# An mLSTM and feed-forward kernel on one core: the gate rows' broadcast in four transfers, and another order of calls on all engines

## What is computed

```python
def block(x, ctx):
    q, k, v = layernorm(x), ctx, ctx                # 4 heads of 128
    ig, log_fg = gates(q, k, v)                     # per row and head
    cums = cumsum(log_fg)
    log_D = cums[s] - cums[t] + ig[t]               # for t <= s
    m = max_t(log_D)
    C = (q @ k.T / sqrt(128)) * exp(log_D - m)
    h = C @ v / (max(|sum_t C|, exp(-m)) + 1e-6)    # per head
    x = x + headnorm(h) * outnorm_weight
    y = layernorm(x)
    g = silu(bitlinear(y, w_gate)) * bitlinear(y, w_up)    # 512 -> 2048
    return x + bitlinear(g, w_down)                 # 2048 -> 512
```

## Time and profile before

| | us |
|---|---|
| median of 3 runs | 712.29 |
| lowest, highest | 709.3, 714.63 |
| profiled execution, own time | 717.73 |
| its span, first to last instruction | 716.0 |
| PE busy (matmuls) | 595.0 (83%) |
| DVE busy | 532.6 (74%) |
| ACT busy | 495.5 (69%) |
| POOL busy | 302.6 (42%) |
| mean granted TensorE clock | 0.95 |

### The profile page before, as it was taken

How to read it: one execution, slowest core, us unless ns; L and a number is a source line. 1 busy time by engine, 2 the same in 40 slices (tenths; PEclk the granted TensorE clock), 3 DMA queues, 4 the chain that set the end, 5 groups by cost and what they waited for, 6 DMA issues and landing times. The chain is left out here.

```text
span 716.0 us, 12756 instructions
## 1 busy us (share of the span) xinstructions
PE 595.0 (83%) x3630; PEld 385.9 (54%) x3630; DVE 532.6 (74%) x1390; ACT 495.5 (69%) x812; POOL 302.6 (42%) x489
## 2 busy tenths in 40 slices
PE   1816548798898889898898889897999989789996
PEld 1806435376456655565456645664656655456442
DVE  3159477767987688857897798869886699689863
ACT  1877864687758766777659776877577775875652
POOL 1126455554444535535435445444444356144200
PEclk9999658899999999989999999999998999999999
DMA  8763414000142111510242123310160031000001
GB/s 337 310 232 127 171 73 164 16 27 20 75 162 75 45 69 38 204 44 0 74 161 73 44 74 100 135 44 7 68 219 30 15 148 44 19 13 15 32 15 45
DMA packets 30752, 63.75 MB, mean 89 GB/s; under 512 B 2304, under 2 KB 18816, under 8 KB 27136
## 3 DMA queue, kind: packets, MB, share of 16 engines
q1 hardware_dynamic: 30144, 62.92, 24.2%
q10 hardware_dynamic: 576, 0.44, 0.3%
HBM read 54.84 MB, written 8.52 MB: 88 GB/s over the span
## 5 line engine op out<-in xcount | busy, mean ns | idle before, releaser
L556 PE MATMUL GU<-WQ,xqT 128*128 128x512 bf16 x1024 | 245.3, 388 | 4.4 <-DVE FF L1153 4.3
L556 PEld LDWEIGHTS GU<-WQ,xqT 128*128 128x128 bf16 x1024 | 99.7, 100 | 109.2 <-issue 12.5
L586 PE MATMUL ACC<-WQ,FF 128*128 128x512 bf16 x512 | 117.4, 383 | 2.2 <-ACT FF L818 2.2
L799 ACT ACTIVATE FF<-GU,cgu 128x512 f32<-128x512 f32 x128 | 86.4, 688 | 25.2 <-PE GU L556 23.2
L1153 DVE TENSOR_TENSOR FF<-FF,GU 128x512 f32<-128x512 f32 x128 | 85.2, 681 | 12.0 <-ACT FF L799 8.7
L807 ACT ACTIVATE FF<-FF,magic,hs 128x1024 f32<-128x1024 f32 x64 | 78.7, 1237 | 15.7 <-DVE hs L1184 15.7
L586 PEld LDWEIGHTS ACC<-WQ,FF 128*128 128x128 bf16 x512 | 50.0, 99 | 59.4 <-ACT FF L818 2.6
L504 PE MATMUL AT<-vext,CT 128*128 128x129 f32 x256 | 56.5, 306 | 6.1 <-ACT gate_parts L697 3.8
L571 PE MATMUL TPB<-ident,FF 128*128 128x128 bf16 x512 | 40.2, 223 | 23.4 <-DVE FF L1195 18.8
L765 ACT ACTIVATE work<-AT,pb 128x128 f32<-128x128 f32 x128 | 47.8, 450 | 13.9 <-POOL pb L1448 13.3
L1455 POOL TENSOR_TENSOR work<-work,norm_bc 128x512 f32<-128x512 f32 x32 | 41.8, 1305 | 35.9 <-ACT work L765 35.9
(11 more groups left out here) (114 smaller groups left out, 1234.1 us busy)
## 6 DMA issues: line engine op xcount, KB each, us to landing
bc<-gate_rows SPq DMA_DIRECT2D x8, 2048.0 KB, 7.5
xin<-in_x SPq DMA_DIRECT2D x32, 256.0 KB, 2.8
kT<-in_ctx_t SPq DMA_DIRECT2D x8, 1024.0 KB, 4.9
vext<-in_ctx SPq DMA_DIRECT2D x32, 256.0 KB, 3.7
out<-FF SPq DMA_DIRECT2D x32, 256.0 KB, 2.3
WQ<-in_w_gate SPq DMA_DIRECT2D x4, 1024.0 KB, 12.6
FF<-in_w_up SPq DMA_DIRECT2D x4, 1024.0 KB, 15.3
FF<-in_w_down SPq DMA_DIRECT2D x4, 1024.0 KB, 4.7
```

The costliest lines, as they stand in the source:

```text
L556: last = nc.tensor.matmul(dst, xqT[:, b, P * k:P * (k + 1)], w[:, k, 512 * j:512 * (j + 1)], start=(k == 0), stop=(k == KC - 1))
L586: last = nc.tensor.matmul(ACC[:, :], hT[:, b % 2, P * k:P * (k + 1)], WD[:, k, :], start=(k == 0), stop=(k == JT - 1))
L799: nc.scalar.activation(sg[:, j % 2, :], GU[:, 2 * (j % 2), :], ACT.Silu, scale=cgu[:, b, 0:1]).then_inc(silu_done, 1)
```

## The change

The broadcast of the gate rows becomes four calls spread_rows(g, b), each with the four rows of a batch (512 KB on the chip), a semaphore of its own and a wait for its own batch's last readers only. Its readers (exp_decay, weigh_q) wait for their batch; exp_rows waits for all four. spread_small is split into keep_floor(g) and keep_decay(g, b). The lists of calls are written in another order on all five engines; the two ring tables are written from another starting point, and their cyclic order is the same. The work and the depth of the pipeline are the same.

```diff
-        bc_in = sem("bc_in")
+        bc_in = [sem(f"bc_in{b}") for b in range(B)]
...
 
-            def spread_rows(g):
...
-                rows_out_at, ct_ready_at = values(sp, (g + 1) * 16, g * 4)
+            def spread_rows(g, b):
+
+                if absent(g):
+                    return
+                n = g * 4 + b
...
-                             rows_dram.rearrange("r n -> (r n)").partition_broadcast(P)).then_inc(bc_in, 16)
+                r = slice(NH * b, NH * (b + 1))
+                sp.dma_start(bc[:, r, :, :].rearrange("p r k t -> p (r k t)"),
+                             rows_dram[r, :].rearrange("r n -> (r n)").partition_broadcast(P)).then_inc(bc_in[b], 16)
 
...
-                if absent(g):
-                    return
-                dve.wait_ge(bc_in, (g + 1) * 16)
-                V.tensor_copy(decay[:, :], bc[:, :, 1, P - 1]).then_inc(dve_seq, 1)
+            def keep_floor(g):
+                if absent(g):
+                    return
+                V.tensor_copy(floor_n[:, :], cols[:, 2, :]).then_inc(dve_seq, 1)
                 count.next()
-                V.tensor_copy(floor_n[:, :], cols[:, 2, :]).then_inc(dve_seq, 1)
+
+            def keep_decay(g, b):
+                if absent(g):
+                    return
+                dve.wait_ge(bc_in[b], (g + 1) * 16)
+                r = slice(NH * b, NH * (b + 1))
+                V.tensor_copy(decay[:, r], bc[:, r, 1, P - 1]).then_inc(dve_seq, 1)
                 count.next()
```

The order on SP (a part), and on POOL:

```diff
+                step = step_of(it)
                 oldest, former, now, coming = it - 2, it - 1, it, it + 1
+                load_x(now, 3)
+                spread_rows(former, 3)
                 load_x(coming, 0)
+                if step == 0:
+                    load_weights(0, w_gate)
+                load_v(former, 3)
+                if step == 0:
+                    load_weights(1, w_up)
                 if step == 1:
                     load_quarter(2, w_down, 0)
                     load_quarter(2, w_down, 1)
                     load_quarter(2, w_down, 2)
                     load_quarter(2, w_down, 3)
+                load_k(coming)
                 load_v(now, 0)
-                if step == 0:
-                    load_weights(1, w_up)
+                spread_rows(now, 0)
+                spread_rows(now, 1)
+                store(oldest, 0)
                 load_x(coming, 1)
-                load_k(coming)
+                load_v(now, 1)
+                store(oldest, 1)
                 load_x(coming, 2)
-                store(oldest, 1)
-                load_v(now, 1)
-                spread_rows(now)
-                load_x(coming, 3)
+                spread_rows(now, 2)
                 store(oldest, 2)
+                store(oldest, 3)
                 load_v(now, 2)
-                if step == -1:
-                    load_weights(0, w_gate)
-                load_v(now, 3)
-                store(oldest, 3)
-                store(former, 0)
 
             for it in range(-1, FULL):
                 iteration(it)
...
+                weigh_keys(former, 2)
+                head_scale(former, 1)
                 x_rstd(coming, 0)
-                head_scale(former, 1)
+                mask_scores(now, 1)
                 residual(former, 1, slot_former)
                 weigh_keys(former, 3)
                 x1_rstd(former, 1)
                 head_scale(former, 2)
+                mask_scores(now, 2)
                 residual(former, 2, slot_former)
-                weigh_keys(now, 0)
                 x1_rstd(former, 2)
                 head_scale(former, 3)
-                x_rstd(coming, 1)
+                weigh_q(now, 0)
                 residual(former, 3, slot_former)
                 x1_rstd(former, 3)
-                weigh_q(now, 0)
                 weigh_q(now, 1)
+                weigh_keys(now, 0)
+                x_rstd(coming, 1)
                 x_rstd(coming, 2)
+                mask_scores(now, 3)
                 x_rstd(coming, 3)
+                weigh_q(now, 2)
+                head_scale(now, 0)
+                weigh_q(now, 3)
+                residual(now, 0, slot_now)
                 mask_scores(coming, 0)
-                weigh_q(now, 2)
+                x1_rstd(now, 0)
                 weigh_keys(now, 1)
-                mask_scores(coming, 1)
-                head_scale(now, 0)
-                weigh_keys(now, 2)
-                weigh_q(now, 3)
-                mask_scores(coming, 2)
-                residual(now, 0, slot_now)
-                x1_rstd(now, 0)
-                mask_scores(coming, 3)
```

More of the change, by code:

```diff
@@ L1274, in iteration @@
+                state_update(former, 2)
+                multiply(former, 0, 2)
+                copy_hT(oldest, 3)
                 if step == 0:
                     weight_round(0, 0)
-                x1_scale(former, 1, slot_former)
-                copy_cols(now)
-                multiply(former, 0, 1)
+                x_norm(coming, 0, slot_coming)
+                if step == 0:
+                    weight_round(0, 1)
+                x1_stats(former, 2, slot_former)
                 if step == 0:
@@ L1291, in iteration @@
                 h_scale(former, 0)
-                x1_scale(former, 2, slot_former)
-                if step == 0:
-                    weight_round(0, 2)
-                multiply(former, 1, 0)
                 multiply(former, 1, 1)
                 x1_stats(former, 3, slot_former)
+                x1_scale(former, 3, slot_former)
+                result(oldest, 3, slot_oldest)
+                x_stats(coming, 2, slot_coming)
+                keep_decay(now, 0)
+                keep_decay(now, 1)
@@ L1298, in iteration @@
+                multiply(former, 1, 2)
                 state_update(former, 3)
[L1299 removed]
                 x_norm(coming, 1, slot_coming)
[L1301 to L1308 removed]
```

320 lines of the change are left out of this document (158 added, 162 removed).

## The result

The changed kernel takes 672.69 us in the median (672.03 to 673.65, 4 runs), the kernel before 712.25 in the runs beside it (709.3 to 714.63, 4 runs): ratio 0.9447, 95% interval [0.9409, 0.9486]. It is 5.5% faster. The forecast of 690 had the sign right, and its outer range (672 to 712) holds the time by 0.7 us only; the range given for case A, 680 to 698, did not hold it, and case C (675) came nearest.

What follows compares the result with a forecast made beforehand. PE's own work, 68.5 us a round, was taken as the floor, with only its idle to win. −25.6 (idle) + 6 (start) − 2 (clock) = −21.6: 696 us from the profiled 717.7, 690 from the median 712.3; range 672 to 712.

Steps and rivals of the forecast that it cites:

- case A: The forecast itself holds for the whole kernel: 680 to 698 us, chance 0.57.
- case C: More than the forecast: walk too careful and half the clock loss goes, −32 + 3 − 8, 675 us; chance 0.15.
- What bounds it: PE's work is the floor, 68.5 us a round; 7.8 us idle can be won, the largest wait from POOL's queue order.
- The six rounds: In the six full rounds PE's idle falls from 7.8 to 3.3 us a round: 25.6 us less, ends 0 and 45.4.
- The prediction's walk: One round followed through all four queues with the profile's durations: 3.3 us of PE idle left in 71.8 us.
- The clock: Six rounds lose 14 us to PE's granted clock of 0.97; fewer waits win back 2, ends 0 and 10.
- The drain: The stretch after the full rounds has no new work and few such waits: 0, ±3 us.
- The start: ACT's new order delays copy_qT(2) by 3.6 us and exp_rows(0) by 4.9: +6 us at the first gate_up, ends 0 and +9.
- The broadcast: Four parts and their earlier issue, with the split decay copies, are worth 0; ends −1 and +3 us in all.
- ACT's exp_decay(2) ahead of copy_qT(2): transpose_xn(3) waits for a table load and four exps, 1.28 us each, yet costs 0; by the skill page some 8 us worse.
- B: DVE takes over: POOL stretches its operations, DVE fills the round at 74.5 us; 703, or 708 with less won; chance 0.17.
- D: Slower by new waits in a line: x_norm(1) behind state_update(3) slides transpose_xn(1) and score(0); 727 us, chance 0.11.

Runs made afterwards that it cites:

- The last version: The changed kernel with ACT's old order in the first iteration (weight sums between the first scores, weight_divide behind exp_rows): 667.4 us, 0.9346.
- the version with two moved calls: The kernel before with POOL's residual(0) ahead of mask_scores(2) and PE's gate_up(2,1) ahead of score(1): 674.27 us, 0.9454.

## Why the prediction was right, and where it was not

**What bounds it: right.** PE's own work is the floor (68.5 us a round before, 68.1 after), and the largest wait came from POOL's queue through DVE. The version with the residual first shows it by moving one call (−4.2%), the one with the masks back by the reverse (+24.6 us).

**The six rounds: right in kind, too careful in size.** The prediction's walk gave a round of 71.8 us, measured 71.05; its idle 3.3 us, measured 2.9. The walked waits and the measured ones: numerators(0) 0.55 and 0.33, numerators(1) 0.35 and 0.33, numerators(2) 1.6 and 1.48, the last two xq transposes 0.15 each and 0.30 and 0.43; the 0.25 before state_step(1) and before numerators(3) did not show. −25.6 was forecast for PE's idle, −28.3 came; the term for the round as such was −31.5. Of the 5.9 us between, some 2.2 are idle (2.9 for 3.3 us a round), 2.0 PE's busy time (68.13 for 68.47), and 1.4 that six undisturbed rounds would have held 46.8 us of idle, not 45.4.

**The clock: the step that failed.** "With fewer waits of PE some of it may go: I take 2 of the 14, with ends 0 and 10." Nearly all of it went: 12.4 us by the length of the rounds, about 13.5 of the 15.6 by PE's busy time, outside the given ends. The prediction took the loss as given and did not ask which waits brought it. The trace of before already gave a hint: the five stretches that begin in the rounds begin at one of two waits (the front's 0.69 and 1.11, and the 3.22), and both were to go by the walk. Had each stretch been put beside the row that it follows, a term near −12 could have been stated, on the condition that the shorter waits of the walk bring none; that they don't is what the changed kernel showed. Case C had some of it (8), and no case had all.

**The drain: not forecast.** "0, ±3", measured −5.5: 3.1 of PE's busy time, which is the clock again (0.97 before, with stretches at 615.6 and 707.8 us that the changed kernel does not have), and 2.4 of idle. The version with the front's wait put back shows how one wait at the turn to the drain (2.81 for 0.50 us) moves it.

**The start: right.** +6 forecast at the first gate_up; +4.8 there (116.6 for 111.7 us) and +5.0 at the first full round. Its parts came as forecast too: 3.3 us for 3.6 at copy_qT(2), 4.4 for 4.9 at exp_rows. The last version takes it back with ACT's order alone.

**The broadcast: right for this order, wrong as a statement of its own.** "I take 0 for all of it": one broadcast in place of four made no difference to the rounds of the new order. In the old order the parts cost 0.8%, and two early ones 3.4%. The term had priced the landing and the issues and not what stands behind them in SP's queue and the DMA queues, nor what an earlier weigh_q does to DVE beside it. In this change neither mattered: nobody in its rounds waits for a load of x or for a part. For the load of x(1), which stands behind two parts on SP, that is luck, since the prediction had not looked at it.

**ACT's exp_decay(2) ahead of copy_qT(2): right.** None of PE's waits in the round is at transpose_xn(3). The Trainium skill (ScalarE: Activation LUTs, What ACT_TABLE_LOAD costs) gives about 2.66 us for a switch; the start's rows above show 1.28 and 0.01 us behind it.

**The rivals.** B (DVE takes over, 703) did not come: DVE is busy 62.2 of 71.1 us, its x_norm takes 0.54 or 0.55 us at all four places, and PE waits for it at one place, 1.48 us. B's own sum does not fit together: a round of 74.5 us is 1.8 below 76.3, not 2.5, and would have given 707. D (727) did not: the slide of x_norm(1) behind state_update(3) is not in the list of waits. C was nearest, by its mechanism too ("half the clock loss goes"), and had 0.15.

**The sum.** Against the profiled execution: −31.5 (undisturbed rounds) − 12.4 (clock) + 5.0 (start) − 5.5 (drain) = −44.4, as measured; forecast −21.6. So 10.4 of the 22.8 us between them are the clock in the rounds, 5.9 the rounds as such, 5.5 the drain and 1.0 the start. In medians the change is −39.6, since the profiled execution of before lay 5.4 us above its median.

What stays open: how much of the 10.9 us of the moved gate_up is the wait itself and how much the clock was read from stretches and lengths, not forced; and why one round gets a stretch behind a wait and the next, with the same wait, does not.

## What to carry to other kernels

Look first for a queue in which a call stands and waits for something that the call behind it doesn't need: here two lines swapped on POOL gave three quarters of the whole gain, and a third moved on PE gave the rest. Put each half-clock stretch beside the wait that it follows, and price that wait with the slower work behind it, not only with its own length; where two waits can bring it, filling one won nothing here that 10 runs could tell. A transfer moved forward or split is priced by what is queued behind it, and the order of a pipeline's start deserves its own look, since here it cost back 5 to 6 us that the rounds had won.

## What the runs showed of the hardware

- TensorE's granted clock fell to about half, 1.2 GHz, behind waits as short as 1.1 us (with one of 0.69 us 6 us ahead) in a kernel whose PE is 83% busy, for 3.4 or 6.8 us at a time; in the kernel before two of five such fronts and three of five waits of 3.2 us were followed by it. With no wait over 1.5 us in a round no stretch began in the six rounds of the changed kernel, nor in those of the version with two moved calls.
- 512 KB of broadcast took 4.7 us to land in the changed kernel and 5.9 with four in a row; 2 MB took 7.5 to 7.9. Four parts in a row were there 9.1 us after the first issue.
- A 256 KB load issued 1.4 us behind 1 MB of broadcast was there after 6.1 us; the median of such loads in the kernel before is 2.8.
- A DVE subtraction of 128x512 took 1.41 us beside a POOL multiply of the same size and 0.48 without it.
